# Attention stage of a four-layer kernel: side work in blocks, rows issued by the sync engine, q and k parts laid out by column

## The reference

```
h = _layernorm(x, axis=-1) * (1 + ca) + sa
qkv = (h @ w_qkv).reshape(Bx, Tx, 3, H, HD)            # 16 sequences, 512 tokens, 16 heads of 16
scores = einsum('bhqd,bhkd->bhqk', q, k) * SCALE       # causal
scores = scores + head_scales * q_proj[..., :, None] * k_proj[..., None, :]
attn = softmax(scores);  out = (attn @ v) @ w_out
x = x + ga * out
```

## Time and profile before

| | us |
|---|---|
| median of 3 runs (2677.25 to 2684.58) | 2678.53 |
| the profiled execution | 2683.27 |
| its span, first to last instruction | 2681.3 |
| PE busy in the span | 2320.9 |
| DVE busy | 1624.2 |
| ACT busy | 1314.3 |
| POOL busy | 435.1 |

### The profile page before, as it was taken

How to read it: one execution, slowest core, us unless ns; L and a number is a source line. 1 busy time by engine, 2 the same in 40 slices (tenths; PEclk the granted TensorE clock), 3 DMA queues, 4 the chain that set the end, 5 groups by cost and what they waited for, 6 DMA issues and landing times. The chain is left out here.

```text
span 2681.3 us, 45165 instructions
## 1 busy us (share of the span) xinstructions
PE 2320.9 (87%) x15010; PEld 1680.5 (63%) x15010; DVE 1624.2 (61%) x3570; ACT 1314.3 (49%) x2260; POOL 435.1 (16%) x364
## 2 busy tenths in 40 slices
PE   7999999998799996588888888888888875169997
PEld 6666667666688884455555555555555565158996
DVE  4666767675444546656666666665666555766664
ACT  3565656564445554555555554555555543034442
POOL 0000000000111114210000000000000022046664
PEclk8999999999899997799989998999999987579998
DMA  4300000000000001232222222332222128145542
GB/s 113 110 0 0 0 0 0 0 0 17 15 0 0 0 0 39 50 81 76 77 71 74 72 73 70 73 76 71 72 72 72 38 92 280 47 130 123 127 93 32
DMA packets 122975, 156.64 MB, mean 58 GB/s; under 512 B 26896, under 2 KB 104096, under 8 KB 122784
## 3 DMA queue, kind: packets, MB, share of 16 engines
q1 hardware_dynamic: 104480, 129.85, 17.7%
q0 software_dynamic: 14336, 25.44, 4.9%
q10 hardware_dynamic: 4096, 0.53, 0.1%
HBM read 96.26 MB, written 58.98 MB: 58 GB/s over the span
## 5 line engine op out<-in xcount | busy, mean ns | idle before, releaser
L1386 DVE TENSOR_REDUCE at_top<-psum 128x1 f32<-128x512 f32 (+3 forms) x1024 | 456.7, 484 | 346.9 <-PE psum L1122 346.6
L1567 ACT ACTIVATE out_x<-psum 128x512 f32<-128x512 f32 (+1 forms) x768 | 385.4, 536 | 449.5 <-PE psum L1140 448.1
L1120 PE MATMUL psum<-out_x 96*128 96x512 bf16 (+3 forms) x1024 | 292.9, 312 | 59.5 <-DVE at_top L1386 42.3
L1138 PE MATMUL psum<-out_x 98*128 98x512 bf16 (+3 forms) x1024 | 289.0, 309 | 60.9 <-DMA out_x<-at_neg_top 37.8
L1122 PE MATMUL psum<-at_mask_q,at_ident_b 128*128 128x128 bf16 x1024 | 205.0, 226 | 0.0
L1120 PEld LDWEIGHTS psum<-out_x 96*128 96x128 bf16 x1024 | 102.6, 100 | 162.4 <-DVE at_top L1386 105.1
L1140 PE MATMUL psum<-at_mask_k,at_ident_b 128*128 128x128 bf16 x1024 | 202.5, 224 | 0.0
L1138 PEld LDWEIGHTS psum<-out_x 98*128 98x128 bf16 x1024 | 101.5, 99 | 159.3 <-issue 70.8
L1156 PE MATMUL psum<-out_x,at_values 128*32 128x512 f32 (+3 forms) x2048 | 165.7, 467 | 0.8 <-ACT out_x L1567 0.8
L2360 POOL DMA_INDIRECT out<-ex_result,slot_tokens x64 | 119.5, 1868 | 102.9 <-DVE ex_result L2492 88.3
L1156 PEld LDWEIGHTS psum<-out_x,at_values 128*32 128x32 f32 x2048 | 64.1, 116 | 94.3 <-issue 79.0
(11 more groups left out here) (400 smaller groups left out, 5896.1 us busy)
## 6 DMA issues: line engine op xcount, KB each, us to landing
out_x<-qk_parts SPq DMA_DIRECT2D x128, 192.0 KB
out_x<-qk_parts SPq DMA_DIRECT2D x128, 128.0 KB
qk_parts<-at_q_parts SPq DMA_DIRECT2D x96, 128.0 KB
qk_parts<-at_k_parts SPq DMA_DIRECT2D x96, 128.0 KB
x_residual<-in_x SPq DMA_DIRECT2D x16, 512.0 KB, 3.9
out_x<-qk_parts SPq DMA_DIRECT2D x128, 64.0 KB
token_rows<-ro_h_tok SPq DMA_DIRECT2D x16, 512.0 KB, 3.0
token_rows<-ro_gate_row SPq DMA_DIRECT2D x16, 512.0 KB, 4.1
```

The lines of the kernel that those rows point to most:

```text
L1120: pe.matmul(out, q_stack[0:STACK, h, qt * P:(qt + 1) * P], k_stack[0:STACK, h, 0:w], start=True, stop=True)
L1138: pe.matmul(bank(bk)[:, col:col + w], k_stack[0:STACK + N_SHIFT, h, kt * P:(kt + 1) * P], q_stack[0:STACK + N_SHIFT, h, kt * P:T], start=T ...
L1386: dve.tensor_reduce(top[:, h, qt:qt + 1], bank(MAX0 + n % 2)[:, col:col + w], AX.X, ALU.max).then_inc(mxr.sem, 1)
L1567: act.activation(probs[:, slot(h), 512 * f:512 * f + w], bank(f)[:, 0:w], ACT.Exp).then_inc(ex.sem, 1)
```

## The change

Five things change, all in attention.

1. `dve_batch` and `act_batch` do a head's side work after all three fills of the head; several pieces move to another step. On PE `pe_turn_max` comes after the third fill of its step, and the second `pe_turn_delta` one step earlier.
2. The rows of maxima are issued by SP (`sp_row`) at written-out places between stores and loads; load 1 no longer waits for row 2. Only row 0 of batch 0 stays on ACT.
3. The columns of the q and k weights are permuted when they are split, so that a partition holds column c of head h at 8c + h within its half of the heads.
4. `qk_parts` in DRAM has the order side, part, half of the heads, column, head, token, and a side is stored in one DMA.
5. The loads read four heads of one half; a row of a load is four heads of 512 tokens, 4 KB, as before.

```diff
-N_STORES = 2 * 3 * 2
+N_STORES = 2
+M_HEADS = P // HD
...
-        parts_dram = nc.dram_tensor("qk_parts", (2, 3, HD, HEADS, T), BF16, kind="Internal").ap()
+        parts_dram = nc.dram_tensor("qk_parts", (2, 3, DK, HD, M_HEADS, T), BF16, kind="Internal").ap()
...
-                    if f == 1 and h % GROUP == 1 and not (last and h + GROUP > HEADS):
+                if h % GROUP == 1 and not (last and h + GROUP > HEADS):
...
-                if h == 12 and not first:
+                if h == 11 and not first:
                     pe.wait_ge(*xs(i - 1, 1))
                     pe_turn_delta(pe, i - 1, 1)
...
         def dve_batch(dve, i, first, last, norm):
             for h in range(HEADS):
-                for f in range(3):
-                    if h + AHEAD < HEADS:
-                        dve_max(dve, i, h + AHEAD, (f,))
...
-                    if h == 12 and f > 0 and norm:
-                        dve_norm(dve, i + 2, False, (2 * f - 2, 2 * f - 1))
...
+                if h == 15 and norm:
+                    dve_max(dve, i + 1, h + AHEAD - HEADS, (0, 1))
+                    dve_hT_lo(dve, i + 2)
+                    dve_max(dve, i + 1, h + AHEAD - HEADS, (2,))
+                elif h + AHEAD < HEADS:
+                    dve_max(dve, i, h + AHEAD)
+                elif not last:
+                    dve_max(dve, i + 1, h + AHEAD - HEADS)
+                if h % GROUP == 1 and not (last and h + GROUP > HEADS):
+                    g = h // GROUP
+                    dve_neg_max(dve, *((i, g + 1) if g + 1 < NG else (i + 1, 0)))
+                if h in (0, 1) and not last:
+                    for n in range(2):
+                        dve_qk_rest(dve, i + 1, 2 * h + n)
+                if h == 4 and not first:
+                    dve_normal(dve, i - 1, 3, SIDE_B)
+                if h == 6 and not first:
+                    dve_o_lo(dve, i - 1)
+                if h == 7:
+                    dve_normal(dve, i, 0, SIDE_B)
...
+                if h == 8 and norm:
+                    dve_stats(dve, i + 2)
+                    dve_moments(dve, i + 2)
+                if h == 12 and norm:
+                    dve_norm(dve, i + 2)
+                if h == 13:
+                    dve_normal(dve, i, 2, SIDE_A)
...
         def act_batch(act, i, first, last, turn):
             for h in range(HEADS):
                 for f in range(3):
                     act_exp(act, i, h, f, first)
...
-                    if f == 0 and h % GROUP == 2 and not (last and h + GROUP > HEADS):
-                        g = h // GROUP
-                        act_row(act, *((i, g + 1) if g + 1 < NG else (i + 1, 0)))
...
+                if h in (0, 1) and not last:
+                    for n in range(2):
+                        act_qk(act, i + 1, 2 * h + n)
+                    for n in range(2):
+                        act_qk2(act, i + 1, 2 * h + n)
+                if h == 3 and not last:
+                    act_values(act, i + 1)
...
+                if h == 14 and turn:
+                    for k in range(DK):
+                        act_hT(act, i + 2, k)
+                    for k in range(DK):
+                        act_hT_hi(act, i + 2, k)
...
-            for j in range(3):
-                for m in range(2):
-                    sp.dma_start(parts_dram[side, j, :, 8 * m:8 * m + 8, :].rearrange("c h t -> h c t"),
-                                 qk_parts[side][:, j, m, :]).then_inc(stored.sem, 16)
+            sp.dma_start(parts_dram[side].rearrange("j m c h t -> (c h) (j m) t"),
+                         qk_parts[side][:, :, :, :].rearrange("p j m t -> p (j m) t")).then_inc(stored.sem, 16)
...
-            elif g == 1:
-                sp.wait_ge(*(loaded[0](0, loaded[0].per) if isinstance(b, int) and b == 0 else row[2](b - 1, row[2].per)))
+            elif g == 1 and isinstance(b, int) and b == 0:
+                sp.wait_ge(*loaded[0](0, loaded[0].per))
             for side, n, parts in LOADS:
-                src = parts_dram[side, parts, :, GROUP * g:GROUP * (g + 1), :]
+                h0 = GROUP * g % M_HEADS
+                src = parts_dram[side, parts, g // 2, :, h0:h0 + GROUP, :]
...
+        def sp_row(sp, b, g):
+            sp.wait_ge(*neg(b, N_SHIFT * (g + 1)))
+            for j in range(N_SHIFT):
+                sp.dma_start(q_stack[STACK + j:STACK + j + 1, GROUP * g:GROUP * (g + 1), :].rearrange(
+                    "a h (q p) -> a (h q) p", p=P), neg_top[:, j, :]).then_inc(row[g].sem, 16)
+
+        def sp_batch(sp, i, last):
+            sp_row(sp, i, 1)
+            if not last:
+                sp_store(sp, i + 1, 0)
+                sp_store(sp, i + 1, 1)
+            sp_row(sp, i, 2)
+            if not last:
+                sp_load(sp, i + 1, 0)
+                sp_load(sp, i + 1, 1)
+            sp_row(sp, i, 3)
+            if not last:
+                sp_load(sp, i + 1, 2)
+                sp_row(sp, i + 1, 0)
+                sp_load(sp, i + 1, 3)
```

More of the change, by code:

```diff
@@ new lines, in dve_batch @@
+                if h in (0, 1) and not last:
[7 more added lines that the diff above has]
+                    dve_normal(dve, i, 0, SIDE_B)
+                if h == 10:
+                    dve_normal(dve, i, 1, SIDE_A)
+                    if not first:
+                        dve_add(dve, i - 1, 0)
@@ L1489, in _ @@
+                if h == 11 and not first:
+                    dve_add(dve, i - 1, 1)
+                if h == 8 and norm:
[5 more added lines that the diff above has]
+                    dve_normal(dve, i, 2, SIDE_A)
         @block.vector
@@ L1639, in act_w_hi @@
             f, w = WEIGHTS[n]
-            act.activation(w[0][:, :, :], f, ACT.Copy).then_inc(w_hi, 1)
+            act.activation(w[0], f, ACT.Copy).then_inc(w_hi, 1)
         def act_batch(act, i, first, last, turn):
@@ L1656, in act_batch @@
-                    if h == 2 and f < 2 and not last:
-                        if f == 0:
-                            act_qk2(act, i + 1, 1)
-                        act_qk(act, i + 1, 2 + f)
-                    if h == 3 and f < 2 and not last:
-                        act_qk2(act, i + 1, 2 + f)
-                    if h == 4 and f < 2 and not last:
-                        act_values(act, i + 1, (f,))
-                    if h == 6 and f < 2 and not first:
-                        act_o_hi(act, i - 1, (f,))
@@ L1666, in act_batch @@
-                    if h in (9, 10) and f == 0 and not first:
-                        act_delta(act, i - 1, h - 9)
-                    if turn:
-                        if (h, f) == (14, 1):
-                            act_hT(act, i + 2, 0)
-                        if (h, f) == (14, 2):
-                            act_hT_hi(act, i + 2, 0)
-                        if (h, f) == (15, 0):
-                            act_hT(act, i + 2, 1)
-                        if (h, f) == (15, 1):
-                            act_hT_hi(act, i + 2, 1)
+                if h % GROUP == 0 and not (first and h == 0):
+                    act_keep_oT(act, *((i, h // GROUP - 1) if h else (i - 1, NG - 1)))
@@ new lines, in act_batch @@
+                if h in (0, 1) and not last:
[5 more added lines that the diff above has]
+                    act_values(act, i + 1)
+                if h == 6 and not first:
+                    act_o_hi(act, i - 1)
+                if h in (8, 9) and not first:
+                    act_delta(act, i - 1, h - 8)
@@ L1796, in sp_load @@
                              ).then_inc(loaded[g].sem, 16)
-        def sp_batch(sp, i):
-            for side in range(2):
-                sp_store(sp, i + 1, side)
-            for g in range(NG):
-                sp_load(sp, i + 1, g)
+        def sp_row(sp, b, g):
[17 more added lines that the diff above has]
+                sp_load(sp, i + 1, 3)
         @block.sync
```

59 lines of the change are left out of this document (14 added, 45 removed).

## The result

The changed kernel takes 2720.42 us (median of 4 runs, 2714.85 to 2722.38) against 2678.30 for the one before: a ratio of 1.0149, 95% interval 1.0127 to 1.0171, 42 us more. The forecast was 2690 with 2625 to 2735 about it: the sign was right, the loss 3.7 times the 11.5 us forecast. The profiled execution took 2722.38.

The account below looks back on a forecast made before the run. The prediction took in-order TensorE's work plus its waits to bound the kernel. 24.5 + 39.8 + 2.2 = 66.5 us a batch, +0.7 over 15 batches (+10.5), and +1 at the ends gave 2690 us, range 2625 to 2735.

Parts of the forecast that it names:

- late narrow load 0 at h = 9: PE at head 9 waits some 3.2 us for the next batch's group 0 load, landing 13.7 us after group 2's maxima.
- rival 3: Every PE wait of about 1 us lowers the clock: 72.1 us a batch, 2773 us in all; chance 15%.
- the clockwork of B: From head 12's first scores to the next batch's group 2 maxima, side work in blocks gives 39.8 us at full clock.
- about 0 together: Heads 14 and 15 get shorter, the next head 0 waits 0.9 us for ScalarE: no net change.
- what replaces row 2's wait: PE's 1.94 us wait at head 8 for group 2's maxima goes; waits at heads 9 and 12 come instead.
- row 3 behind two loads: Group 3's row of maxima, queued after two loads, lands 24.5 us after group 2's maxima, so PE waits at head 12.
- 66 x 0.16 = 10.6 us: Packet time of a narrowed load: 66 packets on the busiest engines at 0.16 us; issue to landing 12.6 us, against 10.6.
- A: Stretch from the end of group 2's maxima to head 12's first scores: 24.5 us forecast, some 23.3 before in the mean.
- the clock in B: From head 12 to the next group 2 maxima, 1.3 low-clock visits a batch cost 2.2 us (bounds 0 and 6.8).
- sum of 66.5: Forecast us for a batch in the attention loop: 24.5 + 39.8 + 2.2, +0.7 a batch.
- the ends: Outside the loop: batch 0's first load lands 1.9 us later, the last batch gains about 1; together +1.
- Stores. Worth 0: Twelve stores become two, done some 8 us before the next load may go: worth 0.

Follow-up runs that it names:

- all_wide: The changed kernel with k's layout giving wide k loads and q's broadcasts issued as six DMAs of 16 rows each: 2570.0 us, ratio 0.9593.
- k_wide: The changed kernel with qk_parts ordered so that k loads are wide again and a side is stored in two DMAs: 2646.4 us, ratio 0.9877.
- rows_all_wide: The kernel of all_wide with the rows of maxima issued by ScalarE again: 2619.4 us, ratio 0.9768.
- before_columns: The kernel before with only the new column layout, two stores and narrow loads; side work and rows as before: 2637.7 us, ratio 0.9856.
- rows_act: The changed kernel with the rows of maxima issued by ScalarE again and the second load waiting for group 2's row again; narrow loads stay: 2634.8 us, ratio 0.9842.
- load0_first: The changed kernel with the next batch's first load issued ahead of group 2's row of maxima on SyncE: 2670.8 us, ratio 0.9948.

## Why the prediction came out as it did

The wait that was named, for a late narrow load 0 at h = 9, is the one that the runs show; its size was not, and errors of both signs met in the sum. 2720.4 lies in 2625 to 2735 but above the forecast's own 2670 to 2715: the room above that was kept for rival 3, in which every wait of 1 us lowers the clock, and that is not what happened. That the range held is in part luck.

**Right, with luck: the clockwork of B.** At full clock B was forecast at 39.8 by hand, head by head; all_wide and k_wide, which have no low level in B, show 39.79 and 39.80, and most batches of the change 39.8. The waits of about 1 us stand where they were put: 1.01 at h = 13 for DVE, 0.96 at h = 0 for ScalarE, 0.59 at h = 1 and 2. From before to all_wide, h = 2 and 3 became 1.03 us shorter (forecast 1.0), h = 12 became 1.59 shorter (1.5), h = 13 became 1.13 longer (1.0) and h = 5, up to the maxima, 0.47 shorter (0.5). But the forecast's terms add up to -2.0, which makes 40.2; the -2.3 of its sum holds 0.3 that no term gives. The heads h = 14, 15 and 0, set at "about 0 together", became 0.44 shorter, and that fills the gap.

**Right: what replaces row 2's wait.** PE waits at h = 9 for load 0, no longer at h = 8, and row 3 behind two loads is level with PE at h = 12 (0.61 us of wait in the mean). A load's narrow part runs at two or three engines' share, and k's narrowing from 39 packets to 66 on the busiest is what makes the late load cost 74 us more than the wide one does (k_wide).

**Wrong: the term "66 x 0.16 = 10.6 us" for a load's packets.** Spans from the first to the last packet, medians over the loads of the loop that run alone: before 8.7 us for 39 packets, after 11.8 for 66; pairs in the change 22.9, where 21.1 was forecast. The same rule gives 6.2 for the load of before, and the rows at hand said 8.6 for it (1565.9 to 1574.5): the price of a packet was taken from the quiet end of the load, the beginning was left out. The 10.6 us from issue to landing that were read for the load of before, plus 27 more packets at 0.16, would have made 14.9; 14.8 were measured in the mean. With load 1's 0.75 and an issue 0.3 later, load 0 landed not 13.7 but some 16.2 us after the maxima in the mean, and the wait was 5.5 instead of 3.2. With the low clock behind it A became 26.95 instead of 24.5.

**Wrong: the clock in B.** 1.3 visits of the lower level a batch, 2.2 us, were set there. B is 40.27 in the mean, 0.5 over 39.8, and only two of the thirteen stretches B have a visit. Sums around the two:

```profile
1602.60:1606.00 3.40, 3.40 (x24) 1.08 (x20) 0.65 (x2) 0.15 (x1) 0.00 (x0) 0.50 0.36 96
1940.52:1943.92 3.40, 3.40 (x24) 1.05 (x28) 0.77 (x3) 0.27 (x1) 0.00 (x0) 0.50 0.48 93
```

They follow waits in h = 0 that were longer than usual (1.53 us at 1601.06, 1.76 at 1939.09), though a longer one, 1.97 at 1737.12, was followed by none. The regular waits, 0.97 in h = 0 and 1.01 in h = 13, lowered the clock in no batch of the loop; the standing still at h = 9, 5.5 us in the mean, did in each. In rows_all_wide, where the wait in h = 0 is 1.65 us in each batch, a visit lies there in every batch from 2 to 14, which is most of the gap between 0.97 and 1.00 above. In the sum of 66.5 the visits set too high hid 1.7 us of the one in A: 67.25. A slip in the reading of before had little part in it: from 1399.8 to 1860.5 three visits follow h = 3, not four.

**Wrong: the ends.** The batch of the loop was carried over to batch 0 with +0.7. It lost 8.7: it has no output of a batch before it, PE comes to h = 9 some 3 us earlier and waits 9.7 there (1172.28) and 3.8 at h = 12. Ahead of it 5.5 were lost instead of 1.9, since not only load 0 of batch 0 comes later (11.16 us of wait, before 8.78) but load 1 too, and 1.7 are gone before load 0 is issued (1090.15, before 1088.48). The last batch was to gain 1 and lost 2.9: SyncE issues its row 1 behind load 3, and PE waits 3.2 us at h = 4. Together with 2.3 us after attention, whose cause is open, what these four places lost beyond the forecast is 18 of the 28 us by which the profiled executions differ from the sum.

**Wrong in what it left out: "Stores. Worth 0".** In the change that is true, because row 2 holds load 0. Alone, the two stores with the new layout gain 1.4% (before_columns). The forecast saw that the stores are done 8 us before load 0 goes, and took it for a reason to leave them out; it was the sign that SyncE's order throws 8 us away.

## What to carry to other kernels

When DMAs are moved from one engine's program to another's, each wait of the moved ones now holds everything written behind it: look for the transfer that was ready, and give its slack in us before and after. Multiply a packet's price by a count only after the same product has given the length of a transfer that the trace shows whole. A change whose parts gain one by one can lose as a whole; the place to look is where one part uses up the slack that another needs.

## What the runs showed of the hardware

**A packet takes longer when sixteen engines work on sixteen rows.** Two engines alone move 49 GB/s, 0.16 us for a packet of 4 KB. Sums of three stretches: in the change while a DMA of 16 rows runs beside narrow ones, in all_wide over two loads, and in all_wide over the first DMA of the first of them, 16 rows with no other DMA beside it:

```profile
1538.00:1539.00 1.00, 1.00 (x21) 0.69 (x14) 0.00 (x0) 0.10 (x1) 0.25 (x1) 1.00 0.95 115
```

```profile
1500.30:1510.00 9.70, 8.68 (x87) 5.34 (x85) 7.65 (x23) 5.11 (x11) 0.73 (x1) 1.00 0.65 162
1500.36:1500.82 0.46, 0.46 (x8) 0.38 (x6) 0.46 (x2) 0.46 (x2) 0.00 (x0) 1.00 0.54 143
```

In the first, sixteen engines at a share of 0.95 move 115 GB/s, about 0.5 us for a packet; in the second, at 0.65 for 162 GB/s, it is some 0.26. The Trainium skill, "SBUF — State Buffer", section "Door 1: The DMA port swizzle", says that four neighbouring partitions share a port, so that 16 rows reach four ports; with its 32 bytes at 850 MHz a port that would be 109 GB/s, an estimate from the page. The 115 lie near it, the 143 of the third stretch do not: over so short a transfer the estimate is no limit here, and why the same form is slower in the change is open. Either way a load of 12 such packets on each engine spans 4.8 us against 11.8.

**A shared issuing program can cost more than the issue time.** The Trainium skill, "DMA: Bandwidth & Descriptors", section "Issuing engines are not separate DMA queues", says that DMAs on several engines save only the sequencer's time for issuing. For the transfers that may be so; but rows_act and the change differ by 86 us, and 50 of them come back when load 0 no longer stands behind row 2 (load0_first): the sequencer also holds its later DMAs back while it waits for an earlier one's data. Where loads are short, sharing gains (all_wide against rows_all_wide).

**Some issues take longer behind many packets.** Twelve issues of narrow loads took 11.69 us, eighteen of wide ones 8.30: in the first, the last two issues took 1.9 and 3.0 us instead of 0.4 to 0.7. The two busiest engines have 132 packets of these loads to move, those of all_wide 24 each. That the issues waited for room in a queue is a guess; no run shows it.
